# A two-FFN and attention layer on one core: work lists and PSUM banks taken from one run through the program on assumed lengths

## The reference, cut to what matters

```python
x = x + 0.5 * ffn(LN(x))
x = x + attn(LN(x))
x = x + 0.5 * ffn(LN(x))          # the same weights as the first

def ffn(x):                        # 8 experts, all computed, F = 256
    weights = golden_weights(x @ Wr / temperature)      # 8 per token
    h = silu(x @ Wg[e]) * (x @ Wu[e])
    return sum_e weights[e] * (h @ Wd[e])

def attn(x):                       # 16 heads of 16, causal
    q, k, v = x @ Wq.T + bq, x @ Wk.T + bk, x @ Wv.T + bv
    return softmax(mask(q @ k.T / 4)) @ v @ Wo.T + bo
```

## Time and profile before

| | us |
|---|---|
| median of 3 runs | 823.6 (821.93, 823.6, 824.05) |
| the profiled execution | 822.55 |
| its span, first to last instruction | 820.8 |
| TensorE busy in the span | 767.7 (94%) |
| VectorE busy | 477.1 (58%) |
| GpSimd busy | 417.6 (51%) |
| ScalarE busy | 342.1 (42%) |
| mean granted TensorE clock | 0.991 |

### The profile page before, as it was taken

How to read it: one execution, slowest core, us unless ns; L and a number is a source line. 1 busy time by engine, 2 the same in 40 slices (tenths; PEclk the granted TensorE clock), 3 DMA queues, 4 the chain that set the end, 5 groups by cost and what they waited for, 6 DMA issues and landing times.

```text
span 820.8 us, 13838 instructions
## 1 busy us (share of the span) xinstructions
PE 767.7 (94%) x4878; PEld 608.1 (74%) x4878; DVE 477.1 (58%) x1314; ACT 342.1 (42%) x657; POOL 417.6 (51%) x499
## 2 busy tenths in 40 slices
PE   6787998989999999998999998899999999999998
PEld 6566877957768767676777766667777777888887
DVE  5657774485657654669654575955556732455333
ACT  4243434515347344264543454444435443332222
POOL 3465555535555453463544554445355555556663
PEclk9799999999999999999999999999999999999999
DMA  5524432533333413122431331245313212223332
GB/s 174 188 83 154 135 109 71 158 84 106 100 86 98 136 59 105 51 93 91 125 119 40 110 85 59 78 136 137 83 43 113 78 48 98 78 78 107 110 98 70
DMA packets 60805, 81.56 MB, mean 99 GB/s; under 512 B 8384, under 2 KB 44608, under 8 KB 60736
## 3 DMA queue, kind: packets, MB, share of 16 engines
q1 hardware_dynamic: 58544, 80.36, 31.8%
q10 hardware_dynamic: 2192, 0.32, 0.2%
HBM read 67.78 MB, written 12.71 MB: 98 GB/s over the span
## 4 chain that ended last, share of the span: by engine, by line
PE 71%; DVE 12%; issue 4%; POOL 4%; ACT 3%; DMA 1%; SPq 1%; POOLq 0%; ACTq 0%; DVEq 0%
PE gu L478 12%; PE gu L479 11%; PE gu L480 11%; PE dn L500 6%; PE dn L501 6%; PE dn L502 6%; PE ra L611 4%; PE ra L584 4%; PE ra L599 4%; DVE junk L997 2%; PE ra L455 2%; DVE hid L941 1%; DVE hid L949 1%; DVE stats L915 1%; POOL hid L1085 1%
## 5 line engine op out<-in xcount | busy, mean ns | idle before, releaser
L1085 POOL TENSOR_TENSOR hid<-hid,wb 128x512 f32<-128x512 f32 x124 | 160.6, 1295 | 182.5 <-DVE hid L949 182.1
L478 PE MATMUL gu<-xt_hi,wgu_hi 128*128 128x512 f32 x512 | 230.5, 450 | 13.4 <-DVE hid L941 8.2
L1089 POOL TENSOR_TENSOR ht_lo<-hid,ht_hi 128x512 fp32r<-128x512 f32 x124 | 160.5, 1294 | 142.7 <-ACT ht_hi L728 142.6
L479 PE MATMUL gu<-xt_hi,wgu_lo 128*128 128x512 f32 x512 | 204.3, 399 | 0.0
L997 DVE CUSTOM_DVE_ANT_0 junk<-ra,mask 128x128 bf16<-128x128 f32 (+3 forms) x256 | 124.0, 488 | 136.9 <-PE ra L584 134.7
L480 PE MATMUL gu<-xt_lo,wgu_hi 128*128 128x512 f32 x512 | 203.4, 397 | 0.0
L500 PE MATMUL dn<-wd,ht_hi 128*128 128x256 f32 x512 | 163.3, 319 | 2.9 <-POOL ht_lo L1089 2.9
L941 DVE SCALAR_TENSOR_TENSOR hid<-hid,gu 128x512 f32<-128x512 f32 x125 | 85.6, 685 | 126.4 <-ACT hid L720 125.7
L778 ACT ACTIVATE probs<-ra 128x512 f32<-128x512 f32 x160 | 94.9, 595 | 130.8 <-PE ra L599 130.2
L728 ACT ACTIVATE ht_hi<-hid 128x512 fp32r<-128x512 f32 x124 | 77.9, 628 | 161.0 <-POOL hid L1085 141.4
L501 PE MATMUL dn<-wd,ht_hi 128*128 128x256 f32 x512 | 144.2, 282 | 0.0
(11 more groups left out here) (165 smaller groups left out, 867.3 us busy)
## 6 DMA issues: line engine op xcount, KB each, us to landing
wd<-wd_parts SPq DMA_DIRECT2D x56, 512.0 KB, 3.5
wb<-wts_rows SPq DMA_DIRECT2D x62, 256.0 KB, 3.7
qk_parts<-parts SPq DMA_DIRECT2D x32, 192.0 KB, 2.1
q_st<-qk_parts SPq DMA_DIRECT2D x96, 64.0 KB, 3.2
k_st<-qk_parts SPq DMA_DIRECT2D x96, 64.0 KB, 2.4
wd_parts<-wd SPq DMA_DIRECT2D x8, 512.0 KB, 4.3
x_res<-in_x SPq DMA_DIRECT2D x4, 512.0 KB, 6.5
stage<-in_Wg SPq DMA_DIRECT2D x8, 256.0 KB, 4.5
```

Source lines behind the costliest of these rows:

```text
L478: mm(b_, w_hi, xt_hi[q % 2][:, c, :], start=c == 0, stop=False)
L479: mm(b_, w_lo, xt_hi[q % 2][:, c, :], start=False, stop=False)
L1085: nc.gpsimd.tensor_tensor(tb, tb, wb[m % NWB][:, :], ALU.mult).then_inc(hw_done, 1)
L1089: nc.gpsimd.tensor_tensor(ht_lo[n % NHT][:, :], hidden(n)[:, :], f32(ht_hi[n % NHT][:, :]), ALU.subtract).then_inc(lo_done, 1)
```

## The change

Four things change.

1. **Orders.** `spaced`, `DELAY` and `order_of` go. `schedule()` still gives the target times, but they now only rank the items. A new function `plan()` adds each item once for each engine that handles it (TensorE, ACT, DVE, POOL, SP), with an assumed length, what it needs, whether it holds the port that DVE and POOL share, which bank it takes or frees, and for DMAs a size. `Plan.run()` goes through this program once in assumed time: on each engine it looks for the item that could start soonest, takes among those at most 0.1 us later the one of lowest rank, and lets time pass. The order in which items were taken is each engine's list.
2. **Banks.** The two `gu` and four `ra` banks become one pool of six. At most three are in use by gate and up, at most four by the rest. The bank of each use is chosen in the plan (the one that came free first) and fixed; each bank has one semaphore that counts its releases, and a use waits for the release before its own turn.
3. **Groups.** Within a batch, the groups are 3.7 chunks apart (DENSE), and the maxima 0.22 instead of 0.27 chunks; from batch to batch it stays 4 x 4.55.
4. **Small things.** The down-weight subtractions of experts 0 and 1 go from POOL to DVE. ACT's `bias` item waits for the `lo` of chunk 2; a `max` item of DVE waits for its own fourth-last one, and `junk` is indexed by the number of the maximum; `ln` of block 0 is treated by itself in XN_BEFORE.

The diff, cut to its core:

```diff
-NG, NA = 2, 4
+NBANK, NA, NG = 6, 4, 3
-M0, PERIOD = 27.1, 4.55
-BY_POOL = {"sg": (1, 2), "sd": (0, 1)}
+M0, PERIOD, DENSE = 27.1, 4.55, 3.7
+BY_POOL = {"sg": (1, 2), "sd": ()}
...
-        meet = [M0 + PERIOD * (b * GR + g) for g in range(GR + 1)]
+        meet = [M0 + PERIOD * GR * b + DENSE * g for g in range(GR + 1)]
...
-                put(meet[g] - PERIOD + 0.15 + 0.27 * k if b + g else meet[0] - 2.1 + 0.115 * k, ("max", b, g, k))
+                put(meet[g] - DENSE + 0.15 + 0.22 * k if b + g else meet[0] - 2.1 + 0.115 * k, ("max", b, g, k))
...
-    return spaced({it: t for t, it in at})
+    return {it: t for t, it in at}
...
+FIRST = {"dve": {"t": -1.0, "h": -1.0, "max": 0.0, "sg": 0.0, "sd": 0.0, "stats": -0.2, "route": -0.5},
+         "act": {"t": -1.0, "hi": -0.8, "exp": 0.0, "sg": 0.0, "sd": 0.0},
+         "pool": {"exp": -0.3, "newton": -0.6, "xb": 0.0},
+         "pe": {}, "sp": {}}
+BEFORE = {"dve": -0.6, "act": -0.5, "pool": -0.5, "pe": 0.0, "sp": 0.0}
+AFTER_END = {"pe": 0.25, "act": 0.15, "dve": 0.12, "pool": 0.12, "sp": 0.0}
...
+        def earliest(key):
+            o = self.ops[key]
+            e = o["eng"]
+            t = max(free[e], ready[key])
+            if o["port"]:
+                t = max(t, busy_port["pool" if e == "dve" else "dve"])
+            if o["takes"]:
+                side = "g" if o["takes"][0] in "gu" else "r"
+                if in_use[side] >= (NG if side == "g" else NA):
+                    return None
+                spare = [x for x in bank_free if x is not None]
+                if not spare:
+                    return None
+                t = max(t, min(spare))
...
+                t0 = min(times)[0]
+                t, key = min((x for x in times if x[0] <= t0 + 0.1), key=lambda x: (self.ops[x[1]]["rank"], x[1]))
...
+            if o["kb"]:
+                pipe = max(end + 1.8, pipe) + o["kb"] / 230.0
+                done = pipe
...
+        add("pe", ("g", n, 0), 0.70, *head, *low, takes=("g", n), then=[("pe", "u", n - 1, 1)] if n else [])
+        add("pe", ("u", n, 0), 0.70, takes=("u", n), then=[("pe", "g", n, 1)])
+        add("act", ("t", n), 0.5, ("pe", "g", n, 1), ("pool", "lo", n - NHID) if n >= 2 * NHID else None)
+        add("dve", ("t", n), 0.6, ("act", "t", n), frees=("g", n))
+        add("dve", ("h", n), 0.6, ("dve", "t", n), ("pe", "u", n, 1), frees=("u", n))
+        add("pool", ("hi", n), 1.25, ("dve", "h", n), ("sp", "wb", m) if m >= NWB else ("act", "wbp", m), port=True)
+        add("pool", ("lo", n), 1.25, ("act", "hi", n), port=True)
+            add("pe", ("d", n, i), 0.355, *([("pool", "lo", n)] + ready if i == 0 else []))
...
+            width = (0.11, 0.118, 0.175, 0.232)
+            time = (0.31, 0.44, 0.57, 0.70)
+            for k in range(GH * QT):
+                add("pe", ("max", b, g, k), width[k % QT], ("sp", "st", b, g), ("pe", "mt") + ago(2) if G >= 2 else None)
+                add("dve", ("max", b, g, k), time[k % QT], ("pe", "max", b, g, k))
...
         def rbank(it):
-            return ra[USE[it] % NA]
+            return ra[BANK[it]]
 
         def emptied(it):
-            return ra_free[USE[it] % NA], USE[it] // NA + 1
+            return ra_free[BANK[it]], TURN[it] + 1
...
-                            if k >= NG:
-                                pe.wait_ge(gu_free, k - NG + 1)
+                            if TURN[use] > 0:
+                                pe.wait_ge(ra_free[BANK[use]], TURN[use])
...
+                        act.wait_ge(lo_done, NHID)
...
+                        k = MAX_USE[it]
+                        if k >= NA:
+                            dve.wait_ge(*emptied(MAX_AT[k - NA]))
```

More of the change, by code:

```diff
@@ new lines, with __init__, add, run @@
+BEFORE = {"dve": -0.6, "act": -0.5, "pool": -0.5, "pe": 0.0, "sp": 0.0}
+AFTER_END = {"pe": 0.25, "act": 0.15, "dve": 0.12, "pool": 0.12, "sp": 0.0}
+FREE_ORDER = ("stats", "var", "newton", "ln", "aln", "wb")
+class Plan:
+    def __init__(self, target):
+        self.target, self.ops, self.next = target, {}, {}
+    def add(self, eng, item, length, *needs, port=False, takes=None, frees=None, holds=None, lets=None, kb=0, more=0.0, then=()):
+        key = (eng,) + item
+        self.ops[key] = dict(eng=eng, item=item, length=length, needs=[n for n in needs if n], port=port, takes=takes, frees=frees,
+                             holds=holds, lets=lets, kb=kb, more=more, then=list(then),
+                             rank=self.target[item] + FIRST[eng].get(item[0], BEFORE[eng]))
+    def run(self, start):
+        last = {}
+        for key in sorted(self.ops, key=lambda k: (k[0], k[1], k[2:])):
+            o = self.ops[key]
+            if o["item"][0] in FREE_ORDER:
+                continue
+            kind = (key[0], key[1])
+            o["follows"] = last.get(kind)
+            last[kind] = key
+        waits, ready, after = {}, {}, {}
+        for key, o in self.ops.items():
+            pre = o["needs"] + o["then"] + ([o["follows"]] if o.get("follows") else [])
+            for n in pre:
+                assert n in self.ops, (key, n)
+                after.setdefault(n, []).append((key, n in o["needs"]))
+            waits[key], ready[key] = len(pre), 0.0
+        open_ = {e: [k for k in self.ops if k[0] == e and waits[k] == 0] for e in start}
+        free = dict(start)
+        busy_port = {"dve": 0.0, "pool": 0.0}
+        bank_free, bank_turn, in_use = [0.0] * NBANK, [0] * NBANK, {"g": 0, "r": 0}
+        held = {}
+        pipe = 0.0
+        BANK, TURN = {}, {}
+        order = {e: [] for e in start}
+        def earliest(key):
+            o = self.ops[key]
+            e = o["eng"]
[10 more added lines that the diff above has]
+                t = max(t, min(spare))
+            if o["holds"] is not None:
+                if held.get(o["holds"], 0.0) is None:
+                    return None
+                t = max(t, held.get(o["holds"], 0.0))
+            return t
+        left = len(self.ops)
+        while left:
+            best = None
+            for e in start:
+                times = [(earliest(k), k) for k in open_[e]]
+                times = [x for x in times if x[0] is not None]
+                if not times:
+                    continue
+                t0 = min(times)[0]
+                t, key = min((x for x in times if x[0] <= t0 + 0.1), key=lambda x: (self.ops[x[1]]["rank"], x[1]))
+                if best is None or t < best[0]:
+                    best = (t, key)
+            assert best, [(e, open_[e][:4]) for e in start]
+            t, key = best
+            o = self.ops[key]
+            e = o["eng"]
+            open_[e].remove(key)
+            order[e].append(o["item"])
+            left -= 1
+            end = free[e] = t + o["length"]
+            if o["port"]:
+                busy_port[e] = end
+            done = end + AFTER_END[e]
+            if o["kb"]:
+                pipe = max(end + 1.8, pipe) + o["kb"] / 230.0
+                done = pipe
+            done += o["more"]
+            if o["takes"]:
+                side = "g" if o["takes"][0] in "gu" else "r"
+                b = min((x, i) for i, x in enumerate(bank_free) if x is not None)[1]
+                bank_free[b] = None
+                in_use[side] += 1
+                BANK[o["takes"]], TURN[o["takes"]] = b, bank_turn[b]
+                bank_turn[b] += 1
+            if o["frees"]:
+                side = "g" if o["frees"][0] in "gu" else "r"
+                bank_free[BANK[o["frees"]]] = done
+                in_use[side] -= 1
+            if o["holds"] is not None:
+                held[o["holds"]] = None
+            if o["lets"] is not None:
+                held[o["lets"]] = done
+            self.ops[key]["at"] = t
+            for k, timed in after.get(key, ()):
+                waits[k] -= 1
+                if timed:
+                    ready[k] = max(ready[k], done)
+                if waits[k] == 0:
+                    open_[k[0]].append(k)
+        return order, BANK, TURN
@@ L397, in build @@
         ra_full = sem("ra_full")
-        ra_free = [sem(f"ra_free{i}") for i in range(NA)]
+        ra_free = [sem(f"ra_free{i}") for i in range(NBANK)]
         st_done = sem("st_done")
@@ L466, in _ @@
                         q, e, f, s = n // CB, n % CB // FT, n % FT, kind == "u"
-                        k = 2 * n + s
+                        use = (kind, n)
                         if c == 0:
```

223 lines of the change are left out of this document (178 added, 45 removed), and 4 rows, old and new, of the table DELAY.

## The result

The changed kernel takes 781.5 us (median of four runs, 780.5 to 783.4) against 823.6 us: a ratio of 0.9495, 95% interval 0.9473 to 0.9518, so 42 us less. The forecast was 795 us, range 772 to 820. The direction held, and so did the mechanism of the lists; the size was 28.5 us in the sum and 42 us on the chip. The profiled execution took 783.44 us with a span of 781.7 us, 39.1 us less than the span before. The other 3 us between the medians come from which executions were profiled: this one is the slowest of its four, 1.9 us above their median, and the one before lay 1.0 us under its own.

The account below looks back on a forecast made before the run. TensorE was taken as the bound, busy 767.7 of 820.8 us: its work plus what it loses. Gains of 9 + 5 + 4.5 + 6 + 1 + 3 = 28.5 us gave 795 us, range 772 to 820.

Parts of the forecast that it names:

- the middle: From 200 to 680 us: of 17.5 us idle on TensorE, 6 us, a third, was forecast to go.
- half clock and covered gaps: TensorE's losses outside idle time: 5 us gained from half clock, 3 of 19 us from small gaps that modelled matmul ends cover.
- The start: From 16 to 80 us: new orders put no unready Newton step or routing piece first; 9 of 14.6 us idle go.
- Under 7 us idle: Sign that the forecast is right: TensorE idle under 7 us from 16 to 80 us.
- No clock of 0.50 after 25 us: Sign that the forecast is right: no half clock (1.2 GHz) after 25 us; 5 us of gain was forecast from half clock.
- Banks at nothing beside the new lists: Six-bank pool: a third bank starts gate(n+1) one release earlier; those waits (3.85 and 4.1 us) already counted, nothing added.
- The rival of shared banks: Gate and up wait for attention's banks; sign turns at 0.21 us per chunk, 838 us at 0.4; chance of slower 0.14.
- The start alone (809 us): Rival: the middle's lists are as good or bad as before, only 9 + 5 + 1 us go; chance 0.15.
- The plan comes true (772 us): Rival: floor of 755 us with 1 to 3% on top, 763 to 778, say 772 us; chance 0.15.
- Density and the `sd` move: Closer groups: no gain or loss in the sum; first two `sd` subtractions to VectorE: both ends inside the start's 9 us.
- The 7 instead of 9 us at the start: By the exclusive VectorE/GpSimd port lock, the `sd` move frees little while GpSimd's long passes stay; start gives 7, not 9.
- The added wait of the bias item at nothing: ACT's bias item waits for `lo` of chunk 2, done at 50.7 us, long before its own turn: no cost.

## Why the prediction was right, and where its size was wrong

The result lies in the range, at the lower edge of the 780 to 808 us that the forecast itself was given. Term by term, in TensorE's idle time of the two profiled executions:

| term | forecast | measured |
|---|---|---|
| 16 to 80 us | 9 | 10.3 (14.6 to 4.3) |
| 80 to 200 us | 4.5 | 6.4 (9.7 to 3.4) |
| the middle | 6 | 15.0 (17.5 to 2.5) |
| last stage | 1 | 0.2 |
| half clock and covered gaps | 5 + 3 | 7.4 together |
| before 16 us | 0 | -0.4 |
| sum | 28.5 | 38.9 of the span's 39.1 |

- **The step that was mis-sized is the middle.** "Of 17.5 I take 6, a third ... an assumed length that is off by a few tenths makes new ones" was the reasoning; 15.0 went. The gaps looked scattered and so not removable. The new lists alone, with the old banks, leave 2.3 us of them, however many releasers they had, and the run in which the plan may hold an engine for 1.0 us instead of 0.1 has 16.9. They did not have one cause only: the pool of banks beside the old lists also took away half of them (17.5 to 9.0). The fear of assumed lengths was right for one direction: 30% too short brings 28.4 us of idle time to the middle, 30% too long leaves it at 2.4. How small errors act was not tried.
- **The start** went as forecast in size and reason: GpSimd not idle before Newton, no gate matmul waiting for `t`. "Under 7 us idle" was right (4.3), but the early Newton steps made new waits that no term had. "No clock of 0.50 after 25 us" was wrong. The half-clock time apart from the last microseconds went from 13.7 to 10.2 us (half-clock stretches remain near 16, 51 and 173 us), at most 1.7 us of gain where 5 was forecast; the remaining 5.7 of the 7.4 are then covered gaps, where 3 was forecast. That the two errors nearly cancel is luck.
- **Banks at nothing beside the new lists** was right to 2 or 3 us. The reason given, a third bank, is not what the pool does beside the old lists, where the limits of two and three give one kernel. In the changed kernel's plan a third gate/up bank is held at 5 of 256 uses; that limit alone was not tried beside the new lists.
- **The rival of shared banks** needed 0.21 us per chunk. Gate matmuls waited 0.0 us. It did not occur in the changed kernel; with lengths too short gate matmuls did wait 2.5 us in the middle, 1.9 of it for maxima.
- **The start alone (809 us)** happens to be close to what the pool of banks alone gives (810 us), by another mechanism; new lists for the start only were not tried.
- **The plan comes true (772 us)** was the nearer rival: the result lies between it and the forecast, 9.5 us above the one and 13.5 under the other. The forecast took the price of its list term from the gaps before and did not ask the plan for its own time. That needs no chip: the plan of the changed kernel ends at 774.6 us, with TensorE idle 0.6 us from 200 to 640 us, and the span came out 7.1 us longer. In the six other runs with new lists, the 0.1 us rule, unchanged lengths and the port in the plan, the span is 4 to 7 us above the plan's end. With old lists the plan is no such guide (829.4 against 812.7 us), nor with false lengths (765.3 against 838.7 when too short).
- **Density and the `sd` move** at nothing: right, both. The 7 instead of 9 us at the start, by the lock that the Trainium skill states (SBUF — State Buffer, "SBUF: two separate sides"), did not come about: the start gave 10.3 us, and with both subtractions on GpSimd again it has the same 4.3 us idle.
- **The added wait of the bias item at nothing** was wrong. It was placed by its old time of 115 us; the new list moved it to 43.8 us, where it held ScalarE 3.5 us; what this cost TensorE was not separated from the Newton steps. A step that a new order may move has to be costed at its new place.

## What to carry to other kernels

Where one engine has nearly enough work and its idle time is many small waits with different releasers, suspect the lists: write down what each item needs and how long it takes, run through it once, and do not hold an engine for an item that is not ready. Read the plan's own end before you build the kernel: with the new lists and lengths that fit, it was within 1% of the chip here. Err on the long side in the assumed lengths (30% too long cost 17 us, 30% too short 58), and put every exclusion between engines into the plan. Look then at what the greedy choice takes too early: work that is ready but not needed for long, like the Newton steps here.

## What was not expected of the hardware

The granted clock fell without a long gap. Of the changed kernel, two neighbouring stretches:

```profile
168.00:173.00 5.00, 3.63 (x23) 2.49 (x21) 4.78 (x20) 0.96 (x3) 2.54 (x2) 1.00 1.03 272
173.00:177.00 4.00, 4.00 (x19) 3.09 (x17) 3.36 (x11) 0.21 (x1) 0.83 (x1) 0.57 0.56 149
```

Before the drop TensorE was busy 3.6 of 5 us, and its longest wait there was 0.87 us; then 3.4 us ran at 1.2 GHz. In the kernel before, the three drops at the start followed waits of 2.1 to 4.1 us. And the run with lengths too long had 20 us more at half clock than the changed kernel, and its busy time is 6.8 us longer. An estimate of what the clock took, half of the 20 us, is up to 10 us, so the clock can account for all of these 6.8. Waits cost more than the idle-time column says when the clock falls behind them.
